# Attention and quantised FFN on one core: due times of a hand-planned instruction order, and two counters

## The chip, the cores and the metric

One NeuronCore of a Trainium2 chip runs the whole program in one launch. The metric is the device time of one execution in microseconds; lower is better. The time before is the median of three runs.

## The reference

`x` is 4 x 512 x 1024 (2048 tokens), a context of 64 more tokens goes with each of the 4 batches. With `LN` a layer norm without weights:

```python
n = LN(x);  hidden = concat([ctx, n], axis=1)              # 576 keys per batch
q = n @ Wq.T (16 heads of 96);  k, v = hidden @ Wk.T, hidden @ Wv.T (4 heads of 96, each for 4 q heads)
x = x + softmax(q k^T / sqrt(96)) v @ Wo.T
xq = fake_quant(LN(x), per row)
h = silu(xq @ fake_quant(w_gate).T) * (xq @ fake_quant(w_up).T)     # 2752 wide
x = x + fake_quant(h, per row) @ fake_quant(w_down).T
```

`fake_quant` scales each row by its largest magnitude over 127, rounds to whole numbers and scales back. Attention needs near-fp32 accuracy, so each fp32 operand is carried as two fp16 numbers (a high and a low part) and a product takes three matmuls.

## The kernel before

The program has two phases with a barrier of all engines between them. `attention_phase` (0 to 1248.6 us of the profile) does the attention of the four batches and, in its gaps, prepares the FFN weights; `ffn_phase` does the FFN on 16 tiles of 128 tokens.

**Attention.** A prologue is followed by four batches of 18 steps (`step_order`). Step j holds four score tiles `S` of head j (128 queries by 576 keys), five pieces `PV` of head j - 2, and side work `X`: projections V, Q, K and the output projection WO for this or the next batch. TensorE runs them in the order of `batch_order`. A score tile goes through a chain of engines: VectorE's row maximum (`max`, L1113), ScalarE's two exponentials (`exp`, L1006 and L1012; the second writes fp16 into `p_nat`, which has four slots, so it waits until the transposition of the same tile of the previous head has landed), GpSimd's low part (`low`, L791), and a DMA transposition `turn_p` (L686) into `pT`, which `PV` reads (L922). TensorE's next score tile but one waits for the exponentials. After the last tile of a head `invert` takes the reciprocals of the row sums, `inv_out` stores them to HBM (2 KB), `inv_in` (L697 is its wait) loads them back spread over 96 partitions, and `normalise` multiplies the head's output by them.

**Weights of the FFN.** 52 units (`("w", g)`), 4 during batch 0 and 16 during each of the others; every 13 units are 11 narrow ones (gate and up, 128 x 1024) and 2 wide ones (down, 128 x 2752, done in two halves). A unit is loaded into one of two buffers `w_in` (`stage`, L600); VectorE finds its row scale (`scale`, L1143 to L1154); ScalarE multiplies (`lift`, L976); VectorE takes the rounded numbers out into the one buffer `w_int` (`round`, L1161, which waits until the transposition of the piece before has read it, L1160); SP transposes (`turn`, L641) into `w_t` and stores (`keep`, L652, whose wait for the transposition is put down to that line). A wide piece takes all of `w_t`, so its `turn` also waits (L639) for the stores before it. In batch 0 the same two buffers also stage the fp32 query and output weights; `split` makes their high and low parts (ScalarE L962, VectorE L1066), and `cache` stores both for the later batches.

**The order.** Every engine runs one list in order, and a wait at its head holds all that is behind it. `pe_times` gives each TensorE operation a start and an end from fixed costs (`COST`, `S_COST`); `stage_events`, `token_events` and `engine_events` give every other step a due time as an offset from these; the steps of each engine are then sorted by due time. SP's list holds all DMAs of the attention phase. `weight_units` sets when units are due: unit i of batch b at `START[b] + (i + 0.4) * length / UNITS[b]`. Planned time is shorter than real time: batch 3 is planned from 786.7 to 1019.8, and its last output projection ends at 1232 us of the profile.

**Counters.** `w_up` (ScalarE) and `w_out` (VectorE) count both the lifts and rounds of units and the splits, so a wait on either is for a number in the joint order of `STAGE` (`ups`, `freed`).

**The end.** After its list SP waits for the last stores of `keep`. In `ffn_phase` TensorE spreads the scales (L1413) and ScalarE copies them (L1445); SP waits for the stores of `x2` (`store_x`, L722), loads the first token tile (L1307, `ln_tile`) and the quantised weights; VectorE normalises and quantises the tile (L1468 on), a transposition follows, and then the gate matmuls (L1391) start.

Of the kernel before, what the change touches and what calls it, by code (L numbers as in the profile page):

```python
# [1 line left out]

# [67 lines left out]
CUT = 11 * P  # L70
HALF = QC * D // 2
UNITS = (4, 16, 16, 16)

KEYS = [("K", c, h) for c in range(QC) for h in range(2)]
VALUES = [("V", ST - 1)] + [("V", s) for s in range(TT)]
# [112 lines left out]
def weight_units():  # L188

    g, units = 0, []  # L190
    for b in range(B):
        for i in range(UNITS[b]):
            units.append((START[b] + (i + 0.4) * (START[b + 1] - START[b]) / UNITS[b], ("w", g)))
            g += 1
    return units

# [20 lines left out]
    return halves_of(i[1] % NUNIT) if i[0] == "w" else 1  # L217


def ups(i, half=0):  # L220

    return sum(item_halves(k) for _, k in STAGE[:ITEM[i]]) + half + 1


def freed(n):
    return ups(STAGE[n][1], item_halves(STAGE[n][1]) - 1)


def smalls(g, k):
# [8 lines left out]
    return (k - parity + 1) // 2  # L238


def stage_events():

    act, dve, sp = [], [], []
    done = {}
    for n, (t, i) in enumerate(STAGE):
        if n < FIRST:
            done[n] = 0.0
            continue
        load = max(done[n - 2] + 1.0, t - 24.0)
        sp.append((load, "stage", n))  # L250
        t = max(t, load + 5.0)
        if i[0] == "w":
            g = i[1]
            if item_halves(i) == 1:
                dve += [(t, "scale", g, 0), (t + 6.0, "round", g, 0)]
                act.append((t + 3.0, "lift", g, 0))
                sp += [(t + 8.0, "turn", TURNS.index((g, 0))), (t + 12.0, "keep", TURNS.index((g, 0)))]
                done[n] = t + 6.5
            else:
                k = TURNS.index((g, 0))  # L260
                dve += [(t, "scale", g, 0), (t + 3.0, "scale", g, 1), (t + 9.0, "round", g, 0), (t + 15.0, "round", g, 1)]
                act += [(t + 6.0, "lift", g, 0), (t + 9.0, "lift", g, 1)]
                sp += [(t + 10.5, "turn", k), (t + 15.0, "keep", k), (t + 16.5, "turn", k + 1), (t + 21.0, "keep", k + 1)]
                done[n] = t + 15.5
        else:
            act.append((t, "split", n))
            dve.append((t + 2.5, "split", n))
            sp.append((t + 4.5, "cache", n))
            done[n] = t + 4.0
    return act, dve, sp  # L270


def token_events(b):

    q = filled_at(b, ("Q", KV - 1, QC - 1)) - 12.0
    act, dve, pool, sp = [], [], [], []
    for t in range(TT):
        s = q + 8.0 * t
        sp += [(s - 7.0, "tokens", b, t), (s + 11.0, "turn_tokens", b, t)]
        dve += [(s, "stats", b, t), (s + 4.0, "norm", b, t)]  # L280
        pool += [(s + 2.5, "power", b, t), (s + 8.0, "tokens_lo", b, t)]
        act.append((s + 5.5, "tokens_hi", b, t))
    sp.append((q + 25.0, "context", b))
    act.append((q + 31.0, "context_hi", b))
    pool.append((q + 32.5, "context_lo", b))
    return act, dve, pool, sp


def engine_events():

    act, dve, sp = stage_events()
    pool = []
    for b in range(B):
        for o in batch_order(b):
            t = END[b, o]
            if o[0] == "S":
                j, k = o[1:]
                dve.append((t + 0.1, "max", b, j, k))
                act.append((t + 1.0, "exp", b, j, k))
                pool.append((t + 3.0, "low", b, j, k))  # L300
                sp.append((t + 5.0, "turn_p", b, j, k))
                if k == TT - 1:
                    dve.append((t + 3.3, "invert", b, j))
                    sp += [(t + 3.8, "inv_out", b, j), (t + 6.5, "inv_in", b, j)]
            elif o[0] == "PV" and o[2] == TT:
                j = o[1]
                dve.append((t + 0.1, "normalise", b, j))
                act.append((t + 1.4, "out_hi", b, j))
                pool.append((t + 2.2, "out_lo", b, j))
                if HEADS[j % G] == G - 1:  # L310
                    sp.append((t + 4.0, "move_o", b, j // G))
            elif o[0] == "X" and o[2] == parts(o[1]) - 1:
                u = o[1]
                if u[0] == "WO":
                    dve.append((t + 0.1, "add", b, u))
                else:
                    act.append((t + 0.1, "evac", b, u))
                    dve.append((t + 1.6, "evac", b, u))
                if u[0] == "Q" and u[2] == QC - 1:
                    sp.append((t + 3.2, "move_q", b, u[1]))  # L320
                if u == ("WO", KV - 1, TT - 1, 0) or u == ("WO", KV - 1, TT - 1, 1):
# [12 lines left out]
    for n, (b, kv, h) in enumerate(OUT_USES):  # L334
        if b:
            sp.append((filled_at(*out_done(n - 2)) + 0.3, "out_w", n))
    return [sorted(e, key=lambda x: x[0]) for e in (act, dve, pool, sp)]


# [45 lines left out]
def attention_phase(nc, x, ctxT, wqT, wkT, wvT, woT, w_gu, w_dn, x2, inv_d, wq_c, wo_c, gu_q, dn_q, kept):  # L385
    with ExitStack() as ctx:
# [54 lines left out]
        e_in = [sem(f"e_in{i}") for i in range(2)]  # L441
        e_up = sem("e_up")
        e_out = sem("e_out")
        w_up = sem("w_up")
        w_out = sem("w_out")
        w_small = sem("w_small")
# [91 lines left out]
        def staged(eng, n):  # L538

            eng.wait_ge(w_in_s[n % 2], (n // 2 + 1) * EV)  # L540

        def split_to(n):

            kind, *a = STAGE[n][1]
            if kind == "wv":
                cols = slice(a[0] * HALF, (a[0] + 1) * HALF)
                return wv_hi[:, cols], wv_lo[:, cols]
            if kind == "q":
                slot = (a[0] * QC + a[1]) % 2
                return wq2[:, slot, 0, :], wq2[:, slot, 1, :]  # L550
            return wo2[:, a[1], 0, :], wo2[:, a[1], 1, :]
# [31 lines left out]
        def _(sp):  # L583
            def stage(n):

                if n >= 2:
                    sp.wait_ge(w_out, freed(n - 2))
                kind, *a = STAGE[n][1]
                if kind == "w":
                    q, u = divmod(a[0], NUNIT)  # L590
# [11 lines left out]
            def cache(n):  # L602

                kind, *a = STAGE[n][1]
                sp.wait_ge(w_out, freed(n))
                if kind == "q":
                    slot = (a[0] * QC + a[1]) % 2
                    sp.dma_start(wq_c[a[0], a[1]], wq2[:, slot, :, :]).then_inc(wq_kept[slot], EV)
                else:
                    sp.dma_start(wo_c[a[0], a[1]], wo2[:, a[1], :, :]).then_inc(wo_kept[a[1]], EV)  # L610
# [20 lines left out]
            def turn(k):  # L631

                g, h = TURNS[k]
                rows, _ = unit_part(g, h)
                sp.wait_ge(w_out, ups(("w", g), h))
                first, blocks = turn_blocks(k)
                sp.wait_ge(w_stored[k % 2], stores_before(k, k % 2) * EV)
                if blocks > KD or (k and turn_blocks(k - 1)[1] > KD):
# [170 lines left out]
        def _(pe):  # L809
# [31 lines left out]
            def v_proj(use, part, n):  # L841
                b, (_, s) = use
                if b is None:
                    if part == 0 and s < TT:
                        pe.wait_ge(xn_turned[s], EV)
                    elif s == ST - 1:
                        pe.wait_ge(ctx_lo, 1)
                        pe.wait_ge(w_out, freed(ITEM["wv", part]))
                if part == 0:
                    claim(use)  # L850
                rows = P if s < TT else C
# [6 lines left out]
            def q_proj(use, part, n):  # L858
                b, (_, kv, q) = use
                slot = (kv * QC + q) % 2  # L860
                if part == 0:
# [2 lines left out]
                    elif kv == 0 and q == 0:  # L864
                        pe.wait_ge(e_out, 1)
                    else:
                        pe.wait_ge(w_out, freed(ITEM["q", kv, q]))
                    if kv == 0 and q == 0:
                        for t in range(TT):
                            pe.wait_ge(xn_turned[t], EV if b is None else b * EV + 2 * EV)  # L870
# [6 lines left out]
            def out_proj(use, part, n):  # L877
# [4 lines left out]
                if t == 0:  # L882
                    if b:
                        pe.wait_ge(wo_in[h], ((b - 1) * KV + kv + 1) * EV)
                    else:
                        pe.wait_ge(w_out, freed(ITEM["o", kv, h]))
                claim(use)
                ts = slice(t * P, (t + 1) * P)
                ws = [slice(c * 512, (c + 1) * 512) for c in range(QC)]
# [57 lines left out]
        def _(act):  # L947
            DOWN = 1.0 / W_UP

            def w_split(n):  # L950
# [8 lines left out]
                elif kind == "o" and a[0]:  # L959
                    filled(act, out_done(a[0] * 2 + a[1] - 2))  # L960
                    act.wait_ge(wo_kept[a[1]], a[0] * EV)
                nc.scalar.activation(split_to(n)[0], split_from(n), ACT.Copy, scale=W_UP).then_inc(w_up, 1)  # L962

            def early_split(i):

# [94 lines left out]
        def _(dve):  # L1060
            DOWN = 1.0 / W_UP

            def w_split(n):
                hi, lo = split_to(n)
                dve.wait_ge(w_up, ups(STAGE[n][1]))
                nc.vector.scalar_tensor_tensor(lo, split_from(n), W_UP, hi, ALU.mult, ALU.subtract).then_inc(w_out, 1)  # L1066

            def early_split(i):
                dve.wait_ge(e_up, i + 1)
# [63 lines left out]
            def tile_scale(g, h):  # L1133
# [5 lines left out]
                if h == 0:  # L1139
                    staged(dve, n)  # L1140
                    if g:
                        dve.wait_ge(w_up, ups(("w", g - 1), halves_of((g - 1) % NUNIT) - 1))
                nc.vector.tensor_reduce(w_amax[0:rows, h:h + 1], w_in[0:rows, n % 2, cols], AX.X, ALU.max,  # L1143
                                        apply_absolute_value=True).then_inc(w_small, 1)
                if h < halves - 1:
# [10 lines left out]
            def round_off(g, h):  # L1156
                n, k = ITEM["w", g], TURNS.index((g, h))
                rows, cols = unit_part(g, h)
                dve.wait_ge(w_up, ups(("w", g), h))
                dve.wait_ge(w_turned, k * EV)  # L1160
                nc.vector.tensor_scalar(w_int[0:rows, 0:cols.stop - cols.start], w_in[0:rows, n % 2, cols], MAGIC, None,  # L1161
                                        ALU.subtract).then_inc(w_out, 1)
# [497 lines left out]
```

## Time and profile before

| | |
|---|---|
| median of three runs | 1757.22 us (1755.55 to 1758.23) |
| the profiled execution | 1757.65 us |
| its span, first to last instruction | 1755.9 us |
| TensorE matmul busy | 1567.4 us (89%) |
| VectorE, ScalarE, GpSimd busy | 1036.7, 655.3, 515.5 us |
| DMA moved | 323.6 MB, 77.2% of 16 engines' span |
| mean granted TensorE clock | 0.955 |

In the rows below, L12 is line 12 of the kernel. A timeline row gives start (us), busy time (us), engine, line, operation, what it writes and reads with its shape, and in brackets how long the engine sat idle before it and what ended that. For SP ("SPq") the second number is the time that the queue took to issue the DMA. A row of waits gives who waited for whom: us in total, times, longest. A row by stage gives the stretch, its length, busy us of TensorE's matmuls, its weight loads, VectorE, ScalarE and GpSimd (with counts), the mean granted TensorE clock, the mean busy share of the 16 DMA engines (over 1 where transfers overlap) and GB/s.

### The profile page before, as it was taken

The numbers are of one execution on the slowest core, as the hardware profiler recorded it, in microseconds if no ns is written. First come the engines' busy times: TensorE is split into PE (matmuls) and PEld (weight loads), VectorE is DVE, ScalarE is ACT, GpSimd is POOL, SyncE is SP. The second block draws the span as 40 slices with busy tenths as digits, with TensorE's granted clock in tenths as the row PEclk, the third lists the DMA queues.
The fourth block names the chain that finished last, engine by engine and source line by source line (L and its number), as shares of the span: only waits on it lengthen the run. The fifth ranks groups of instructions, "written<-read, shape, count | busy, mean of one in ns | idle before, by whom it ended". The sixth has DMA issues, their size and how long they took to land. (4 is left out here: it accounts for less than half of the span.)

```text
span 1755.9 us, 23588 instructions
## 1 busy us (share of the span) xinstructions
PE 1567.4 (89%) x8084; PEld 773.3 (44%) x8084; DVE 1036.7 (59%) x1760; ACT 655.3 (37%) x1180; POOL 515.5 (29%) x635
## 2 busy tenths in 40 slices
PE   6989989999877999888799788898579999999997
PEld 3544434654333465443346334443234444444443
DVE  5346554345555434555444445465379999898984
ACT  3456553256544225555422455452211111111110
POOL 3356653045445214445521244452000000000000
PEclk9999999999898999999999899999789999999998
DMA  7499999699999969999986999998863333324232
GB/s 233 116 249 237 240 231 233 185 212 228 226 227 230 200 173 222 239 209 230 222 200 187 263 218 205 207 202 199 263 227 85 91 89 86 95 80 105 70 93 64
DMA packets 546185, 323.62 MB, mean 184 GB/s; under 512 B 484144, under 2 KB 491056, under 8 KB 544944
## 3 DMA queue, kind: packets, MB, share of 16 engines
q1 hardware_dynamic: 546096, 322.49, 77.2%
q8 instruction: 50, 0.82, 0.2%
q14 instruction: 39, 0.32, 0.1%
HBM read 151.78 MB, written 46.79 MB: 113 GB/s over the span
## 5 line engine op out<-in xcount | busy, mean ns | idle before, releaser
L791 POOL TENSOR_TENSOR p_nat<-p_f,p_nat 128x512 f16<-128x512 f32 x256 | 300.6, 1174 | 478.9 <-ACT p_nat L1012 478.4
L1113 DVE TENSOR_REDUCE small<-ps_s 128x1 f32<-128x576 f32 x256 | 192.8, 754 | 257.2 <-PE ps_s L908 255.7
L907 PE MATMUL ps_s<-k,q 96*128 96x512 f16 x768 | 231.2, 393 | 95.4 <-ACT p_nat L1012 95.4
L1006 ACT ACTIVATE p_f<-ps_s,small 128x576 f32<-128x576 f32 x256 | 189.2, 739 | 267.5 <-DVE small L1113 265.5
L1012 ACT ACTIVATE p_nat<-ps_s,small 128x576 f16<-128x576 f32 x256 | 188.5, 736 | 133.3 <-DMA pT<-p_nat 132.7
L1391 PE MATMUL ps_gu<-w_gu_sb,xT 128*128 128x512 bf16 (+1 forms) x1152 | 230.8, 361 | 0.0
L1432 ACT ACTIVATE g_sb<-g_sb,sx 128x512 f32<-128x512 f32 (+1 forms) x128 | 74.5, 582 | 390.6 <-DVE g_sb L1503 331.5
L1404 PE MATMUL ps_d<-w_dn_sb,hT 128*128 128x512 bf16 x704 | 161.5, 383 | 5.4 <-DMA hT<-h_int 5.4
L907 PEld LDWEIGHTS ps_s<-k,q 96*128 96x128 f16 x768 | 76.2, 99 | 201.7 <-issue 82.1
L1391 PEld LDWEIGHTS ps_gu<-w_gu_sb,xT 128*128 128x128 bf16 x1152 | 112.8, 98 | 115.4
L922 PE MATMUL ps_o<-pT,v_lo 128*96 128x512 f16 x320 | 133.4, 417 | 33.0 <-DMA pT<-p_nat 32.9
L908 PE MATMUL ps_s<-k,q 96*128 96x64 f16 x768 | 150.1, 196 | 0.0
L818 PE MATMUL ps_g<-wo,o 128*128 128x512 f16 x384 | 148.9, 388 | 1.1 <-POOL o L797 1.1
L819 PE MATMUL ps_g<-wo,o 128*128 128x512 f16 x384 | 148.6, 387 | 0.0
L820 PE MATMUL ps_g<-wo,o 128*128 128x512 f16 x384 | 148.5, 387 | 0.0
L818 PE MATMUL ps_g<-xnT,wq 128*128 128x512 f16 x384 | 146.3, 381 | 1.4 <-DMA xnT<-xh 0.7
L820 PE MATMUL ps_g<-xnT,wq 128*128 128x512 f16 x384 | 146.2, 381 | 0.0
L819 PE MATMUL ps_g<-xnT,wq 128*128 128x512 f16 x384 | 146.1, 380 | 0.0
L1370 POOL TENSOR_TENSOR rstd<-var_eps,minus_half 128x1 f32<-128x1 f32 x16 | 8.8, 550 | 460.1 <-DVE var_eps L1473 460.1
L1174 DVE SCALAR_TENSOR_TENSOR x_acc<-ps_g,x_acc 128x512 f32<-128x512 f32 x128 | 88.1, 689 | 86.7 <-PE ps_g L820 86.5
L797 POOL TENSOR_TENSOR o<-o_tmp,o 96x512 f16<-96x512 f32 x64 | 75.6, 1182 | 194.8 <-ACT o L1021 194.8
L923 PE MATMUL ps_o<-pT,v_hi 128*96 128x512 f16 x320 | 130.1, 407 | 0.0
(113 smaller groups left out, 2403.6 us busy)
## 6 DMA issues: line engine op xcount, KB each, us to landing
w_in<-w_gu SPq DMA_DIRECT2D x40, 512.0 KB, 4.7
wq<-wq_c SPq DMA_DIRECT2D x36, 512.0 KB, 4.9
wo<-wo_c SPq DMA_DIRECT2D x24, 768.0 KB, 5.6
inv_sum<-inv_d SPq DMA_DIRECT2D x64, 192.0 KB, 3.4
gu_q<-w_t SPq DMA_DIRECT2D x44, 256.0 KB, 4.1
w_in<-w_dn SPq DMA_DIRECT2D x8, 1376.0 KB, 7.1
w_gu_sb<-gu_q SPq DMA_DIRECT2D x3, 2816.0 KB, 12.8
x_acc<-x SPq DMA_DIRECT2D x4, 2048.0 KB, 8.9
```

The costliest lines, as they stand in the source:

```text
L791: nc.gpsimd.tensor_tensor(n[:, S + C:2 * S], f[:, 0:T], n[:, 0:T], ALU.subtract)
L818: nc.tensor.matmul(o, l_hi, r_hi, start=(first and i == 0), stop=False)
L819: nc.tensor.matmul(o, l_hi, r_lo, start=False, stop=False)
L820: mm = nc.tensor.matmul(o, l_lo, r_hi, start=False, stop=(last and i == len(pairs) - 1))
L907: nc.tensor.matmul(o[:, 0:T], l, k2[0:HD, hl, kv, 0:T], start=(i == 0), stop=(i == 2))
L908: mm = nc.tensor.matmul(o[:, T:S], l, k2[0:HD, hl, kv, T:S], start=(i == 0), stop=(i == 2))
L922: nc.tensor.matmul(o, v_lo[:, t, kv, :], p[:, t, :], start=(t == 0), stop=False)
L1006: nc.scalar.activation(p_f[:, t % NF, :], scores(t), ACT.Exp, bias=bias, accum_out=sums[:, j % 2, t:t + 1])
L1012: nc.scalar.activation(p_nat[:, t % NN, 0:S], scores(t), ACT.Exp, bias=bias).then_inc(p_done, 1)
L1113: nc.vector.tensor_reduce(neg_max[:, j % 2, t:t + 1], scores(t), AX.X, ALU.max, negate=True).then_inc(mx_done, 1)
L1391: mm = nc.tensor.matmul(ps_gu[n % NR][:, 0:nu * P], xT[:, k, :], w[:, u0:u0 + nu, k, :], start=(k == 0), stop=(k == KD - 1))
L1404: mm = nc.tensor.matmul(ps_d[h][:], hT[0:rows, c, :], w_dn[0:rows, 4 * h:4 * h + 4, c, :], start=(c == 0), stop=(c == IC - 1))
```

## The change

Only due times and two counters change; every instruction of the computation stays.

- Splits count on new semaphores `h_up` and `h_out`; `w_up` and `w_out` count the units alone (`lifts`, `split_no`).
- A staged load is due `LAND` + 1 = 7 or more ahead of its first use (before 5); a split's `cache` comes 6 after it, 4.5 before.
- A `round` is due 6 or more after the `turn` before it; a `turn` 2.5 after its `round` and 6 after the stores it needs; a `keep` 6 after its `turn` (before: 4, or 4.5 for wide ones).
- `inv_in` is due 10 after the head's last score tile (before 6.5), 6.2 after `inv_out` (before 2.7).
- Token tiles of the next batch start 20 before the end of the query projections (before 12) in steps of 10 (before 8), with 8 between `stats` and `norm` (before 4).
- `out_w` 1.5 after the matmuls that free its buffer (before 0.3).
- In batch 3 the due times of the 16 units are drawn in to 0.85 of its length.

```diff
+WEIGHTS_FOR = (1.0, 1.0, 1.0, 0.85)
...
-            units.append((START[b] + (i + 0.4) * (START[b + 1] - START[b]) / UNITS[b], ("w", g)))
+            units.append((START[b] + (i + 0.4) * WEIGHTS_FOR[b] * (START[b + 1] - START[b]) / UNITS[b], ("w", g)))
...
-def ups(i, half=0):
-
-    return sum(item_halves(k) for _, k in STAGE[:ITEM[i]]) + half + 1
-
-
-def freed(n):
-    return ups(STAGE[n][1], item_halves(STAGE[n][1]) - 1)
+def lifts(g, half=0):
+
+    return sum(halves_of(i % NUNIT) for i in range(g)) + half + 1
+
+
+def split_no(n):
+
+    return sum(1 for _, i in STAGE[:n + 1] if i[0] != "w")
...
+LAND = 6.0
+TOKEN_LEAD, TOKEN_STEP = 20.0, 10.0
...
         load = max(done[n - 2] + 1.0, t - 24.0)
         sp.append((load, "stage", n))
-        t = max(t, load + 5.0)
-        if i[0] == "w":
-            g = i[1]
-            if item_halves(i) == 1:
-                dve += [(t, "scale", g, 0), (t + 6.0, "round", g, 0)]
-                act.append((t + 3.0, "lift", g, 0))
-                sp += [(t + 8.0, "turn", TURNS.index((g, 0))), (t + 12.0, "keep", TURNS.index((g, 0)))]
-                done[n] = t + 6.5
-            else:
-                k = TURNS.index((g, 0))
-                dve += [(t, "scale", g, 0), (t + 3.0, "scale", g, 1), (t + 9.0, "round", g, 0), (t + 15.0, "round", g, 1)]
-                act += [(t + 6.0, "lift", g, 0), (t + 9.0, "lift", g, 1)]
-                sp += [(t + 10.5, "turn", k), (t + 15.0, "keep", k), (t + 16.5, "turn", k + 1), (t + 21.0, "keep", k + 1)]
-                done[n] = t + 15.5
-        else:
+        t = max(t, load + LAND + 1.0)
+        if i[0] != "w":
+            t = split = max(t, split + 3.0)
             act.append((t, "split", n))
             dve.append((t + 2.5, "split", n))
-            sp.append((t + 4.5, "cache", n))
-            done[n] = t + 4.0
+            sp.append((t + 6.0, "cache", n))
+            done[n] = t + 5.0
+            continue
+        g, halves = i[1], item_halves(i)
+        t = max(t, lifted + 1.5)
+        for h in range(halves):
+            dve.append((t, "scale", g, h))
+            t += 3.0
+        for h in range(halves):
+            act.append((t, "lift", g, h))
+            t += 3.0
+        lifted = t
+        t -= 3.0 * (halves - 1)
+        for h in range(halves):
+            k = TURNS.index((g, h))
+            t = max(t, turned[-1] + LAND)
+            dve.append((t, "round", g, h))
+            wide = halves == 2 or (k and halves_of(TURNS[k - 1][0] % NUNIT) == 2)
+            t = max(t + 2.5, (kept[-1] if wide else kept[-2]) + LAND)
+            sp += [(t, "turn", k), (t + LAND, "keep", k)]
+            turned.append(t)
+            kept.append(t + LAND)
+        done[n] = t
...
-                    sp += [(t + 3.8, "inv_out", b, j), (t + 6.5, "inv_in", b, j)]
+                    sp += [(t + 3.8, "inv_out", b, j), (t + 10.0, "inv_in", b, j)]
...
-        s = q + 8.0 * t
-        sp += [(s - 7.0, "tokens", b, t), (s + 11.0, "turn_tokens", b, t)]
-        dve += [(s, "stats", b, t), (s + 4.0, "norm", b, t)]
-        pool += [(s + 2.5, "power", b, t), (s + 8.0, "tokens_lo", b, t)]
-        act.append((s + 5.5, "tokens_hi", b, t))
...
+        s = q + TOKEN_STEP * t
+        sp += [(s - 8.0, "tokens", b, t), (s + 16.0, "turn_tokens", b, t)]
+        dve += [(s, "stats", b, t), (s + 8.0, "norm", b, t)]
+        pool += [(s + 2.5, "power", b, t), (s + 12.0, "tokens_lo", b, t)]
+        act.append((s + 9.5, "tokens_hi", b, t))
...
-                    sp.wait_ge(w_out, freed(n - 2))
+                    freed(sp, n - 2)
...
-                nc.scalar.activation(split_to(n)[0], split_from(n), ACT.Copy, scale=W_UP).then_inc(w_up, 1)
+                nc.scalar.activation(split_to(n)[0], split_from(n), ACT.Copy, scale=W_UP).then_inc(h_up, 1)
```

## Rows read from the trace of the kernel before

**Rows 1.** Stages: us, PE PEld DVE ACT POOL busy, TensorE clock, DMA share, GB/s.
```profile
375.00:602.00 227.00, 192.84 (x972) 91.68 (x970) 115.96 (x184) 114.40 (x210) 109.95 (x136) 0.92 1.04 223
...
965.00:1200.00 235.00, 198.80 (x1032) 96.10 (x1030) 116.51 (x180) 120.56 (x225) 105.46 (x136) 0.93 1.01 219
1200.00:1249.00 49.00, 29.54 (x136) 13.49 (x135) 21.18 (x31) 6.74 (x7) 3.73 (x4) 0.89 0.67 190
```

**Rows 2.** Waits of the matmuls, whole span: total us, times, longest.
```profile
PE ps_s L907 <- ACT p_nat L1012: 95.4, 37, 7.2
PE ps_o L922 <- DMA pT<-p_nat: 32.9, 19, 4.4
```

**Rows 3.** Timeline of VectorE, end of attention and first FFN tile.
```profile
1232.81 0.69 DVE L1174 SCALAR_TENSOR_TENSOR x_acc<-ps_g,x_acc 128x512 f32<-128x512 f32 x1 [1.25 <-PE ps_g L820]
...
1240.07 0.86 DVE L1161 TENSOR_SCALAR w_int<-w_in 128x1344 bf16<-128x1344 f32 x1 [5.77 <-DMA w_t<-w_int]
...
1252.08 1.29 DVE L1468 BATCH_NORM_STATS2 stats<-x_ln 128x6 f32<-128x512 f32 x2 [3.30 <-DMA x_ln<-x]
```

**Rows 4.** Timeline of SP's queue over the same stretch: start, time to issue.
```profile
1233.53 0.38 SPq L722 DMA_DIRECT2D x<-x_acc  x1
...
1245.88 0.33 SPq L652 DMA_DIRECT2D dn_q<-w_t  x1
1248.79 0.33 SPq L1307 DMA_DIRECT2D x_ln<-x  x1
```

**Rows 5.** The chain of waits: first FFN matmuls.
```profile
1262.95 7.81 PE ps_gu L1391 x24
```

**Rows 6.** DMA issues: count, KB each, median us from issue to landing.
```profile
w_in<-w_dn SPq DMA_DIRECT2D x8, 1376.0 KB, 7.1
...
x<-x_acc SPq DMA_DIRECT2D x8, 1024.0 KB, 7.4
...
dn_q<-w_t SPq DMA_DIRECT2D x16, 352.0 KB, 3.5
...
w_t<-w_int SPq DMA_TRANSPOSE x60, 4.5
```

**Rows 7.** Waits of SP's queue, whole span.
```profile
SPq L697 <- DMA inv_d<-small: 40.9, 24, 4.9
...
SPq L652 <- DMA w_t<-w_int: 33.7, 18, 3.8
SPq L639 <- DMA dn_q<-w_t: 20.9, 10, 5.5
```

**Rows 8.** Waits of VectorE, whole span.
```profile
DVE w_int L1161 <- DMA w_t<-w_int: 49.6, 10, 11.0
```

**Rows 9.** VectorE's round of unit 37, batch 3; then the matmuls' waits, 985 to 1010 us.
```profile
999.71 0.86 DVE L1161 TENSOR_SCALAR w_int<-w_in 128x1344 bf16<-128x1344 f32 x1 [10.95 <-DMA w_t<-w_int]
...
PE ps_s L907 <- ACT p_nat L1012: 10.1, 2, 7.2
```

**Rows 10.** SP's queue just before it: start, time to issue.
```profile
986.84 0.55 SPq L679 DMA_DIRECT2D x_acc<-x  x1
987.48 6.79 SPq L686 DMA_TRANSPOSE pT<-p_nat  x1
```

**Rows 11.** ScalarE's split at 111 us; then the matmuls' waits, 100 to 116 us.
```profile
111.49 1.06 ACT L962 ACTIVATE wq<-w_in 128x1024 f16<-128x1024 f32 x1 [7.48 <-DMA w_in<-wqT]
...
PE ps_s L907 <- ACT p_nat L1012: 6.6, 2, 5.7
```

**Rows 12.** VectorE's round at 517 us; then the matmuls' waits, 505 to 535 us.
```profile
516.79 0.86 DVE L1161 TENSOR_SCALAR w_int<-w_in 128x1344 bf16<-128x1344 f32 x1 [5.75 <-DMA w_t<-w_int]
...
PE ps_s L907 <- ACT p_nat L1012: 7.3, 2, 4.6
```

**Rows 13.** VectorE's round at 764 us; then the matmuls' waits, 760 to 770 us.
```profile
763.77 0.86 DVE L1161 TENSOR_SCALAR w_int<-w_in 128x1344 bf16<-128x1344 f32 x1 [6.51 <-DMA w_t<-w_int]
...
PE ps_s L907 <- ACT p_nat L1012: 4.1, 1, 4.1
```

More of the change, by code:

```diff
@@ L238, in stores_before @@
     return (k - parity + 1) // 2
+LAND = 6.0
+TOKEN_LEAD, TOKEN_STEP = 20.0, 10.0
 def stage_events():
     act, dve, sp = [], [], []
-    done = {}
+    done, split, lifted, turned, kept = {0: 0.0, 1: 0.0, 2: 0.0, 3: 0.0}, 0.0, 0.0, [0.0], [0.0, 0.0]
     for n, (t, i) in enumerate(STAGE):
         if n < FIRST:
-            done[n] = 0.0
             continue
@@ L270, in stage_events @@
+        done[n] = t
     return act, dve, sp
 def token_events(b):
-    q = filled_at(b, ("Q", KV - 1, QC - 1)) - 12.0
+    q = filled_at(b, ("Q", KV - 1, QC - 1)) - TOKEN_LEAD
     act, dve, pool, sp = [], [], [], []
     for t in range(TT):
-        s = q + 8.0 * t
-        sp += [(s - 7.0, "tokens", b, t), (s + 11.0, "turn_tokens", b, t)]
-        dve += [(s, "stats", b, t), (s + 4.0, "norm", b, t)]
-        pool += [(s + 2.5, "power", b, t), (s + 8.0, "tokens_lo", b, t)]
-        act.append((s + 5.5, "tokens_hi", b, t))
@@ L283, in token_events @@
-    sp.append((q + 25.0, "context", b))
-    act.append((q + 31.0, "context_hi", b))
-    pool.append((q + 32.5, "context_lo", b))
+        s = q + TOKEN_STEP * t
[3 more added lines that the diff above has]
+        act.append((s + 9.5, "tokens_hi", b, t))
+    s = q + TOKEN_STEP * 2 + 16.0
+    sp.append((s, "context", b))
+    act.append((s + 8.0, "context_hi", b))
@@ L286, in token_events @@
+    pool.append((s + 9.5, "context_lo", b))
     return act, dve, pool, sp
@@ L335, in engine_events @@
         if b:
-            sp.append((filled_at(*out_done(n - 2)) + 0.3, "out_w", n))
+            sp.append((filled_at(*out_done(n - 2)) + 1.5, "out_w", n))
     return [sorted(e, key=lambda x: x[0]) for e in (act, dve, pool, sp)]
@@ L443, in attention_phase @@
         e_out = sem("e_out")
+        h_up = sem("h_up")
+        h_out = sem("h_out")
         w_up = sem("w_up")
@@ L540, in staged, with freed @@
             eng.wait_ge(w_in_s[n % 2], (n // 2 + 1) * EV)
+        def freed(eng, n):
+            kind, *a = STAGE[n][1]
+            if kind == "w":
+                eng.wait_ge(w_out, lifts(a[0], halves_of(a[0] % NUNIT) - 1))
+            else:
+                eng.wait_ge(h_out, split_no(n))
         def split_to(n):
@@ L604, in cache @@
                 kind, *a = STAGE[n][1]
-                sp.wait_ge(w_out, freed(n))
+                freed(sp, n)
                 if kind == "q":
@@ L634, in turn @@
                 rows, _ = unit_part(g, h)
-                sp.wait_ge(w_out, ups(("w", g), h))
+                sp.wait_ge(w_out, lifts(g, h))
                 first, blocks = turn_blocks(k)
@@ L847, in v_proj @@
                         pe.wait_ge(ctx_lo, 1)
-                        pe.wait_ge(w_out, freed(ITEM["wv", part]))
+                        freed(pe, ITEM["wv", part])
                 if part == 0:
@@ L866, in q_proj @@
                     else:
-                        pe.wait_ge(w_out, freed(ITEM["q", kv, q]))
+                        freed(pe, ITEM["q", kv, q])
                     if kv == 0 and q == 0:
@@ L885, in out_proj @@
                     else:
-                        pe.wait_ge(w_out, freed(ITEM["o", kv, h]))
+                        freed(pe, ITEM["o", kv, h])
                 claim(use)
@@ L1064, in w_split @@
                 hi, lo = split_to(n)
-                dve.wait_ge(w_up, ups(STAGE[n][1]))
-                nc.vector.scalar_tensor_tensor(lo, split_from(n), W_UP, hi, ALU.mult, ALU.subtract).then_inc(w_out, 1)
+                dve.wait_ge(h_up, split_no(n))
+                nc.vector.scalar_tensor_tensor(lo, split_from(n), W_UP, hi, ALU.mult, ALU.subtract).then_inc(h_out, 1)
             def early_split(i):
@@ L1141, in tile_scale @@
                     if g:
-                        dve.wait_ge(w_up, ups(("w", g - 1), halves_of((g - 1) % NUNIT) - 1))
+                        dve.wait_ge(w_up, lifts(g) - 1)
                 nc.vector.tensor_reduce(w_amax[0:rows, h:h + 1], w_in[0:rows, n % 2, cols], AX.X, ALU.max,
@@ L1158, in round_off @@
                 rows, cols = unit_part(g, h)
-                dve.wait_ge(w_up, ups(("w", g), h))
+                dve.wait_ge(w_up, lifts(g, h))
                 dve.wait_ge(w_turned, k * EV)
```

## The prediction

> **What bounds the kernel now.** I read the profile from its end. The chain of waits covers only the FFN: its first gate matmuls start at 1262.95 us [rows 5], and from there the chain is TensorE's own work, which the change does not touch. So two things can move: the time that attention takes, and the seam behind it.
>
> At the seam the reader is to see two ends. VectorE's last addition to `x_acc` starts at 1232.81 [rows 3] and SP stores the result at 1233.53 [rows 4]: attention proper is over. Yet the last half of the last weight unit is rounded only at 1240.07, after 5.77 us of waiting for the transposition of the half before [rows 3], its store is issued at 1245.88, and the FFN's first load follows at 1248.79 [rows 4]. The rounding of weights, and not attention, ends the first phase, about 12 us late.
>
> Inside attention the stages show TensorE with 192.8 busy us of 227 in the heads of batch 1 and 198.8 of 235 in those of batch 3, at a mean clock of 0.92 and 0.93 of full, while the 16 DMA engines stand at a share of 1.04 and 1.01; after 1200 us that falls to 0.67 [rows 1]. The matmuls wait 95.4 us for `p_nat`, written by ScalarE behind the transpositions, and 32.9 us for `pT` itself, 128.3 in all [rows 2]. Two causes stand behind these waits and the profile cannot part them by itself: full DMA engines, and lists in which something that nobody needs soon holds up something that TensorE needs. Of the second kind I see: SP waits 40.9 us for the reciprocals to land in HBM, 33.7 us for transposed weights and 20.9 us for stores of weights [rows 7], 95.5 together; VectorE waits 49.6 us in ten roundings of weights [rows 8].
>
> **The change, part by part.** It adds no instruction and no byte. Everything is a matter of place.
>
> *The seam.* Unit 15 of batch 3 was due at 786.7 + 15.4/16 x 233.1 = 1011.1 of the plan; with 0.85 it is 786.7 + 0.85 x 224.4 = 977.4, 34 earlier. The new spacing of wide pieces gives part back: a piece comes every 12 of the plan (6 from its turn to its keep, 6 from that to the next turn), and by the formula the last turn and keep come at 1012.5 and 1018.5 instead of 1027.6 and 1032.1. The plan ends at 1019.8, so the last keep now stands ahead of the last store of `x2`. What ends the phase is then the store at 1233.53. It is not enough that it is issued: the first load of the FFN waits for it to land. The median of its kind is 7.4 us, that of a 352 KB store of weights 3.5 [rows 6], so x2 is there between 1237 and 1241, and the load that was issued at 1248.79 [rows 4] goes out 8 to 12 us earlier; little else is under way there, which speaks for the longer end. Its data is awaited at once (3.30 us idle, VectorE starts at 1252.08 [rows 3]), and from it statistics, transposition and gates follow as before. I take **-10.5 us**. Bounds: -12.7, if the store's landing were hidden by the barrier (1248.79 to about 1236), and 0, if the heads stretch so far that they fill the room.
>
> *Roundings and splits.* Where a wait of this kind stops TensorE can be read at four places. A split waits 7.48 us for its load on ScalarE, and the matmuls near it lose 6.6 us [rows 11]. The second half of a wide unit waits 5.75 us and they lose 7.3 [rows 12]; 6.51 us and 4.1 [rows 13]; 10.95 us and 10.1 [rows 9]. Together 28.1 us. In the new order split 8 stands behind an exponential that it blocked (due 41.8 instead of 38.4, the exponential 39.1), and second halves are due 6 after the transposition they wait for, not 4.5. A weight transposition lands after 4.5 us in the median [rows 6], so 6 is enough for most and not for those that run beside a large load: at the worst place SP took 6.79 us merely to issue a transposition behind the 2 MB residual [rows 10], and only the order of the weight transposition (now 815.6, ahead of the residual's 816.7; before 817.6) is mended there, not the transfer. I take 12 of the 28.1: **-12 us**. Bounds 0 and -28; what is late next at these places is the score tile's own transposition.
>
> *SP's list.* `inv_in` moves 3.5 later; it stood 2.7 behind `inv_out` and now stands 6.2 behind, so most of the 40.9 us [rows 7] goes. `keep` goes from 4 to 6 behind its `turn`, and a wide `turn` from 1.5 behind the last keep to 6; most of 33.7 + 20.9 goes too. A good part of these waits lies in stretches where SP has nothing urgent behind it, and where DMA engines are full a DMA issued earlier mostly lands no earlier. No single place shows TensorE stopped by one of them, so I take little, 8 of the 95.5 us: **-8 us**, bounds 0 and, at half of TensorE's 128.3 us of waits [rows 2], -64. `inv_in` has cover: `normalise` needs it only two steps later, 16 after the last score tile against 10 plus a landing; if that cover goes, `ps_o` is freed late and the next PV waits.
>
> *Tokens, cache, out_w.* The loads of tokens come 1 earlier ahead of their statistics, `norm` 4 later behind them; The last is turned 9 of the plan before the query projections that read it (before 12), which is twice a transposition's 4.5 us [rows 6]: I count nothing, and up to 3 us a batch if that cover goes. The first `turn_tokens` now comes 4 ahead of the matmuls it waits for (before 1): SP then stands up to 4 us three times. Behind it is only the transposition of a score tile from the same time, so nothing is charged. The two counters cost nothing; they allow splits and units to pass each other in batch 0.
>
> *What it costs.* The heads of batch 3 now hold all 16 units. New there are the last 1376 KB load, three wide transpositions and about three stores. By time to landing that is 7.1 + 3 x 4.5 + 3 x 3.5 = 31 us [rows 6], but those overlap other transfers; by share they fall into DMA engines at 1.01 [rows 1], where each microsecond added may push the score transpositions back. Between 0 (all fill gaps) and 31 I take **+8 us**, nearer to the low end, since landing times are mostly latency.
>
> Sum: -10.5 - 12 - 8 + 8 = -22.5 us. Against the profiled execution, 1757.65, that is 1735.15; it stands 0.4 above the median of the runs, so I say **1735**.
>
> [...]
>
> **Rivals.**
> 1. *The DMA engines are the ceiling.* Waits leave SP and VectorE and come back as longer landings. For it: the share in all heads; against it: the places above where a single wait and TensorE's stop coincide. Then only the seam stays, less what the moved transfers cost: 1757.65 - 10.5 + 8 = 1755, within what can't be told from no change, or 1747 if they cost nothing.
> 2. *Slower: batch 3 is overfilled.* The two wide units of the end now fall among score transpositions. The nearest price is the one collision of a wide unit with a large load: the matmuls lost 10.1 us, and the clock fell with it [rows 9]. With each of the two units meeting such a stretch twice, and no relief elsewhere, 1757.65 - 10.5 + 4 x 10.1 = 1787; with one meeting each it is 1767. It is slower from the point where the heads of batch 3 stretch by more than 10.5 + 3.5 = 14 us.
> 3. *SP's list is the true limit.* Half of TensorE's waits go, 64 us instead of 20: 1757.65 - 10.5 - 64 + 8 = 1691. For it: SP takes 6.79 us for a single issue [rows 10], so its list can be full; against it: such an issue is itself a sign of full DMA engines.
> 4. *The order does not do it*: the last keep still ends the phase because wide units lag in real time. SP's relief alone, 1757.65 - 20 + 8 = 1746.
>
> **How the numbers follow.** My own case (1715 to 1749) gets 0.55, rival 1 0.16 (over half of it within 0.2%), rival 2 0.13, rival 3 0.07, rival 4 0.09. Rival 3's far end is left out below, the 1767 and 1787 above; the range is 1710 to 1758. A measurement of this kernel tells about 0.2% (3.5 us) from no change. Slower by more: 0.13; within: 0.10; faster by more: 0.77.
>
> **What would show it.** The last `keep` is issued before or within 3 us of the last store of `x2`, and the first gate matmuls start 10 us and more closer to the last addition (now 30.1 us). SP's wait for `inv_d` falls under 15 us, VectorE's for transposed weights under 25. TensorE's waits fall from 128 to about 105. If SP's waits go and TensorE's stay, rival 1 holds; if the stretch of batch 3's heads grows beyond 249 us, rival 2.

## The result, and the profile after

The changed kernel takes 1696.57 us (median of 4 runs, 1695.48 to 1700.98) against 1756.38 us of the kernel before measured with it: a ratio of 0.9664, 95% interval 0.9644 to 0.9684, or 59 us less by that ratio. Forecast were 1735 us and a range down to 1710; the direction held, the size did not. The profiled execution took 1700.98 us with a span of 1699.3.

First the seam. The timeline of VectorE in the changed kernel, from the last addition of the attention phase:

```profile
1187.91 0.69 DVE L1188 SCALAR_TENSOR_TENSOR x_acc<-ps_g,x_acc 128x512 f32<-128x512 f32 x1 [1.25 <-PE ps_g L834]
...
1196.20 1.29 DVE L1482 BATCH_NORM_STATS2 stats<-x_ln 128x6 f32<-128x512 f32 x2 [6.26 <-DMA x_ln<-x]
```

the timeline of SP's queue over the same stretch (start, time to issue):

```profile
1181.30 0.50 SPq L666 DMA_DIRECT2D dn_q<-w_t  x1
1188.63 0.39 SPq L736 DMA_DIRECT2D x<-x_acc  x1
1192.86 0.34 SPq L1321 DMA_DIRECT2D x_ln<-x  x1
```

and from the chain of waits, the first gate matmuls:

```profile
1206.82 7.37 PE ps_gu L1405 x24
```

The last addition came at 1232.81 [rows 3] and comes at 1187.91: attention is 44.9 us shorter. From it to the gates it was 30.1 us [rows 3, 5] and is 18.9: the seam is 11.2 us shorter. The last keep (1181.30) is now ahead of the last store (1188.63), as the plan said, and the FFN's first load follows 4.2 us behind that store. 44.9 + 11.2 = 56.1, and the profiled executions differ by 56.7. So all of it lies in these two places, and four fifths of the gain lie in attention, where I had expected half.

Attention itself, from the start to the last addition, in rows by stage (columns as in rows 1), before and after:

```profile
0.00:1232.81 1232.81, 1087.54 (x5792) 548.57 (x5792) 611.92 (x941) 571.59 (x1032) 506.66 (x619) 0.95 0.94 215
```

```profile
0.00:1187.91 1187.91, 1076.57 (x5792) 546.59 (x5792) 617.66 (x942) 569.60 (x1032) 511.01 (x619) 0.96 0.96 225
```

The same 5792 matmuls were busy 11.0 us less, at a granted clock of 0.96 instead of 0.95; TensorE's idle time fell by the other 33.9 us. A quarter of what attention gained is thus clock, for which the forecast had no term.

The waits of the matmuls, whole span (total us, times, longest):

```profile
PE ps_s L921 <- ACT p_nat L1026: 68.1, 25, 7.1
PE ps_o L936 <- DMA pT<-p_nat: 20.2, 16, 5.7
```

128.3 us [rows 2] have become 88.3. By stage, the heads of batches 1 and 3 (columns as in rows 1):

```profile
370.00:580.00 210.00, 189.01 (x971) 91.06 (x970) 118.28 (x185) 115.11 (x213) 113.58 (x138) 0.95 1.09 242
925.00:1150.00 225.00, 201.04 (x1057) 98.31 (x1055) 126.01 (x194) 124.55 (x231) 106.34 (x136) 0.93 1.08 247
```

Batch 1's heads run as many matmuls (971 for 972) in 210 us instead of 227 [rows 1], at a clock of 0.95 instead of 0.92, and the DMA share has risen from 1.04 to 1.09 and the rate from 223 to 242 GB/s; in batch 3 the rate went from 219 to 247, there with more of the weight units in the stretch. A share of 1.04 had not meant that the engines could do no more. The score transpositions land a little later than before (median 4.8 us for 4.4), and still TensorE waits less.

The waits of SP's queue, then of VectorE:

```profile
SPq L666 <- DMA w_t<-w_int: 12.0, 7, 3.5
...
SPq L653 <- DMA dn_q<-w_t: 6.0, 2, 4.0
...
SPq L711 <- DMA inv_d<-small: 0.4, 1, 0.4
```

```profile
DVE w_int L1175 <- DMA w_t<-w_int: 52.4, 17, 7.1
...
DVE o_tmp L1145 <- DMA inv_sum<-inv_d: 33.9, 12, 7.4
```

SP's three waits were 40.9 + 33.7 + 20.9 us [rows 7] and are 0.4 + 12.0 + 6.0. VectorE's roundings wait as long as before, 52.4 us against 49.6 [rows 8], though they wait 17 times and at most 7.1 us, not 10 times and up to 11.0. That already contradicts the part of the forecast that was built on them.

One more of SP's waits changed, which neither the rows ahead of the forecast nor the forecast looked at: the wait of `out_w` for the matmuls that free its buffer, before and after.

```profile
SPq L629 <- PE ps_g L820: 43.4, 11, 7.4
```

```profile
SPq L643 <- PE ps_g L834: 15.8, 5, 7.4
```

Before, it was SP's largest wait of the attention phase in total, larger than that for the reciprocals.

### The profile page after: what moved, and what is told of

The parts are those of the page before. It is cut to its first block and busy times, and to the rows that moved or that the text cites. A ratio compares the mean times of both kernels' runs of the same rounds, so it can differ in the third digit from the quotient of the medians.

```text
span 1699.3 us, 23588 instructions
## 1 busy us (share of the span) xinstructions
PE 1554.6 (91%) x8084; PEld 770.8 (45%) x8084; DVE 1040.9 (61%) x1760; ACT 653.1 (38%) x1180; POOL 519.8 (31%) x635
## 5 line engine op out<-in xcount | busy, mean ns | idle before, releaser
L921 PE MATMUL ps_s<-k,q 96*128 96x512 f16 x768 | 227.1, 387 | 68.3 <-ACT p_nat L1026 68.1
L1446 ACT ACTIVATE g_sb<-g_sb,sx 128x512 f32<-128x512 f32 (+1 forms) x128 | 74.6, 583 | 393.1 <-DVE g_sb L1517 335.1
L1026 ACT ACTIVATE p_nat<-ps_s,small 128x576 f16<-128x576 f32 x256 | 188.3, 736 | 37.9 <-DMA pT<-p_nat 37.7
L936 PE MATMUL ps_o<-pT,v_lo 128*96 128x512 f16 x320 | 132.0, 413 | 20.3 <-DMA pT<-p_nat 20.2
```

Of the source, the lines that this page charges most:

```text
L921: nc.tensor.matmul(o[:, 0:T], l, k2[0:HD, hl, kv, 0:T], start=(i == 0), stop=(i == 2))
L936: nc.tensor.matmul(o, v_lo[:, t, kv, :], p[:, t, :], start=(t == 0), stop=False)
L1026: nc.scalar.activation(p_nat[:, t % NN, 0:S], scores(t), ACT.Exp, bias=bias).then_inc(p_done, 1)
```

## The experiments

Three theories. **L**: SP's list was the limit; what holds it holds the score transpositions behind it. Its strong form says that SP has no time to spare at all. **W**: the gain is the new distances of the weight units. **M**: moved transfers meet by luck; parts have no price of their own. Percentages are of the kernel before measured on the same chip, and 1% is 17.6 us.

**The reciprocals alone (e1_inv_only), and all but them (e2_no_inv).**

```diff
-                    sp += [(t + 3.8, "inv_out", b, j), (t + 6.5, "inv_in", b, j)]
+                    sp += [(t + 3.8, "inv_out", b, j), (t + 10.0, "inv_in", b, j)]
```

That is the first, in the kernel before; the second takes the same line back in the changed one.

> The kernel before (1757 us) with inv_in alone due 10 instead of 6.5 after the head's last score tile. Theory L (SP's list was the limit, and its longest hold was the wait for the reciprocals, 40.9 us): 20 us or more of the change's 60, so 1737 us or less, with SP's wait for inv_d near 0 and ScalarE's wait for pT well under the 132.7 us of before. Theory W (the gain comes from the new distances of the weight units): within 5 us of 1757. Theory M (moved DMAs meet by chance in a better way, no part has a price of its own): anything between, and not in proportion to the wait removed.

> The changed kernel (1697 us) with inv_in alone put back to 6.5. L: 1717 us or more, SP's wait for inv_d back near 40 us. W: within 5 us of 1697, though the wait is back.

Alone: 1742.0 us, ratio 0.9896 (0.9857 to 0.9936), 18.3 us less. Taken back: 1719.7 us, 0.9767 (0.9732 to 0.9803), 18.1 us more than the change. W falls as the whole of the cause, and M has its first evidence against it: the part has a price clear of noise in both surroundings. Each price carries some 6 us of doubt, so that they agree to 0.2 us is luck. L's own 20 us were just missed. The waits of ScalarE's second exponential for the transpositions, in the kernel before

```profile
ACT p_nat L1012 <- DMA pT<-p_nat: 132.7, 67, 8.1
```

and in e1:

```profile
ACT p_nat L1012 <- DMA pT<-p_nat: 58.8, 32, 5.0
```

SP's wait for the reciprocals, 40.9 us [rows 7], became

```profile
SPq L697 <- DMA inv_d<-small: 2.5, 5, 1.5
```

38.4 us of SP's waiting went with 73.9 us of ScalarE's and 18.3 us of time. TensorE itself waited only 11.8 us less; the table below takes that up.

**The wait without the move (e8_hold_only).**

```diff
+                    sp += [..., (t + 6.5, "hold", b, j), (t + 10.0, "inv_in", b, j)]
...
+            def hold(b, j):
+                sp.wait_ge(inv_out_s, (head(b, j) + 1) * EV)
```

> The changed kernel, inv_in still issued at 10, but at 6.5 SP also waits, without a DMA, until the reciprocals have landed in HBM. Theory L: the wait itself is the cost, so this is as slow as putting inv_in back (1720 us, 0.9767 of before), with ScalarE's wait for pT near 83 us. If instead the place of the 192 KB load among the transpositions is what cost, this stays within 5 us of 1697.

1712.7 us, 0.9746 (0.9715 to 0.9777): 14.4 us slower than the change, of the 18.1 that the full move is worth. No transfer is added, taken away or reordered against the changed kernel, so most of the price is the wait itself. SP's waits for `inv_d` are 41.4 us in all, put down to what stands behind the hold, most of it to score transpositions:

```profile
SPq L699 <- DMA inv_d<-small: 27.1, 18, 4.1
```

ScalarE's wait for the transpositions, which I expected near 83 us, was only

```profile
ACT p_nat L1030 <- DMA pT<-p_nat: 42.8, 32, 4.3
```

so the path from the held list to TensorE is not the one I had named, or not it alone. What reaches TensorE is in the table below; by which engine it comes stays open.

**How late is too late (e12_inv_late, e14_inv_8).** The changed kernel with `inv_in` due 13 and 8.5.

> The changed kernel with inv_in due 13 after the last score tile. SP's wait is gone already (0.4 us), so L sees no further gain; VectorE's normalise already waits 33.9 us for inv_sum and would wait more: 1700 to 1712 us. If it is faster, the place of the load among the transpositions has a price of its own.

> The changed kernel with inv_in due 8.5. Between the two prices now known (SP waits 39.6 us for the reciprocals at 6.5 and the kernel is 18 us slower; VectorE waits 101.2 us for inv_sum at 13 and it is 26 us slower) there is a best place. SP's wait should come back in part (5 to 12 us, 2 to 6 us of time) and VectorE's fall from 33.9 to about 20: 1692 to 1702 us. If the two are one cost seen twice, the sum is flat: within 3 us of 1697.

13 gave 1725.3 us, 0.9810 (0.9782 to 0.9838), 25.6 us slower than 10, more than expected; the wait of `normalise` in VectorE's list, 33.9 us at 10, became

```profile
DVE o_tmp L1145 <- DMA inv_sum<-inv_d: 101.2, 27, 10.0
```

67 us more of it, while SP waits no less. 8.5 gave 1699.2 us, 0.9671 (0.9645 to 0.9696), no different from 10: SP waits 4.0 us for the reciprocals, VectorE 15.5 for `inv_sum`. The place has a flat floor between 8.5 and 10 and steep sides at 6.5 and 13.

**The weight units (e5_stage_only, e9_wide_close, e6_keep_early, e13_loads_late).** First the due times of loads, splits, rounds, turns and keeps alone, with the two counters:

> Of the change only the due times of loads, splits, rounds, turns and keeps and the two counters; inv_in at 6.5, units spread over batch 3, tokens and out_w as before. If the parts add up, what is left after the reciprocals (18 to 22 us of 60) and the drawn-in units (14) is 25 us, less what tokens and out_w do: 1757 - 20 to - 28, so 1729 to 1737 us. Theory L: SP's waits for w_t and dn_q fall from 54.6 to about 20 us, ScalarE's wait for pT from 132.7 to about 95. Theory M: under 1747 is not reached, the parts only work together.

1741.6 us, 0.9904 (0.9870 to 0.9939): 16.9 us less, 5 us above the range that adding up gave. Then one distance at a time taken out of the changed kernel:

```diff
e9_wide_close
-            t = max(t + 2.5, (kept[-1] if wide else kept[-2]) + LAND)
+            t = t + 2.5
e6_keep_early
-            sp += [(t, "turn", k), (t + LAND, "keep", k)]
+            sp += [(t, "turn", k), (t + 4.0, "keep", k)]
e13_loads_late
-        t = max(t, load + LAND + 1.0)
+        t = max(t, load + 5.0)
```

> The changed kernel, but a turn is due 2.5 after its round whatever stores it waits for, so that the pieces of wide units are 8.5 apart instead of 12. Theory L: SP waits for dn_q (6.0 us) again for 15 to 20 us and the kernel loses 4 to 8 us: 1701 to 1705. If the gain of the due times of the stage (17 us alone) is chiefly this distance, 1708 or more; if it has no price, within 3 us of 1697.

> The changed kernel with each keep due 4 instead of 6 after its turn, all else in place. L: SP waits for w_t again (12.0 goes back to 25 or more) and the kernel loses in the proportion that the reciprocals showed (about 22 us for 40 us of waiting): 5 to 10 us, so 1702 to 1707. M: no price, within 3 us of 1697.

> The changed kernel with a staged load due only 5 ahead of its use, as before, not 7. In batch 0 the splits wait for loads on ScalarE and VectorE again, in front of exponentials and maxima: if that is the price, 3 to 8 us, so 1700 to 1705, all of it in batch 0 and at the wide units. If loads have room anyway, within 3 us of 1697.

e9: 1713.6 us, 0.9759 (0.9733 to 0.9784), 16.7 us slower, nearly all that the weight units are worth. Its SP waits for the stores, 6.0 us in the changed kernel, are

```profile
SPq L653 <- DMA dn_q<-w_t: 25.9, 11, 4.4
```

e6: 1695.5 us, 0.9646 (0.9613 to 0.9679): no price; 6.9 us more of SP's waiting for `w_t` came with 4.3 us less for `dn_q`. e13: 1704.2 us, 0.9696 (0.9671 to 0.9722): 5.6 us, about the width of its interval. L had expected 1702 to 1707 for e6, but SP's waits for landings there came to 20.6 us against 19.6, so that it hardly tests L. Of the three distances tried, one counted, the one in front of a wide `turn`. Taking it out does more than bring the wait back: by the kernel's own due times it also puts 25 of the 60 weight transpositions 1.3 to 14 earlier, closer together. No run parts the wait from the crowding, as e8 did for the reciprocals. The distance of a `round` behind the `turn` before it was not tried alone.

**Batch 3's units spread out again (e3_units_spread).** `WEIGHTS_FOR` all 1.0.

> The changed kernel with batch 3's units spread over its whole length again (1.0 for 0.85). The seam from the last output projection to the first gate matmuls grows from 19.3 us to 30 or more, since the last keep is then about 12 later than before in the plan; attention up to the last output projection gets shorter by up to 8 us if filling batch 3 cost anything. All theories: 1697 + 11 - 8 to + 22, so 1700 to 1719 us.

1713.1 us, 0.9742 (0.9714 to 0.9770), 13.7 us slower. SP's queue at the end:

```profile
1184.94 0.39 SPq L736 DMA_DIRECT2D x<-x_acc  x1
...
1199.69 0.33 SPq L666 DMA_DIRECT2D dn_q<-w_t  x1
1202.55 0.34 SPq L1321 DMA_DIRECT2D x_ln<-x  x1
```

Without the drawing-in, the last store is issued 3.7 us earlier (1184.94 for 1188.63): that is what filling batch 3 costs in these two profiles. The last keep is issued at 1199.69 and the FFN's first load 9.7 us later than in the changed kernel. From the last addition (1184.22) to the gates (1216.55) it is 32.3 us, 13.4 more than there. That is nearly the whole difference of the medians, 13.7, so by these runs filling batch 3 costs from about nothing to some 4 us. The 0.85 alone in the old distances (e4_units_drawn_only) has no time: with those due times the engines' lists wait for one another in a circle.

**The tokens (e7_old_tokens, e15_norm_close).** All due times of the tokens as before; then only those inside a tile (`norm` 4, `tokens_hi` 5.5, `tokens_lo` 8, `turn_tokens` 12 after `stats`), with the new lead and step.

> The changed kernel with the tokens' due times of before. My prediction charged nothing: within 3 us of 1697. If the norm that waits for GpSimd holds VectorE's maxima, 1700 to 1705.

> The changed kernel with the tokens' lead and step kept (20 and 10) but the distances inside a tile as before (norm 4, tokens_hi 5.5, tokens_lo 8, turn_tokens 12 after stats). Old tokens cost 9 us. If the wait of norm for GpSimd (VectorE's list held) was the price, this costs most of it: 1702 to 1707. If it was lead and step (a tile's steps each get more room), within 3 us of 1697.

e7: 1708.2 us, 0.9717 (0.9685 to 0.9749), 9.3 us slower, where I had charged nothing. e15: 1717.6 us, 0.9771 (0.9746 to 0.9795), 18.8 us slower, worse than the old times. `norm` hardly waits for GpSimd in it (5.8 us in all, 4.7 in the changed kernel); what grew, from 29.1 us in the changed kernel, is the wait for the next tile's load in front of `stats`:

```profile
DVE stats L1092 <- DMA xc<-x: 49.5, 7, 10.0
```

`turn_tokens` of tile t is then due at the same time as the load of tile t + 2. That this is why the load comes late is argued, not shown. A second hold is new in e15, SP's in front of the first `turn_tokens` of a batch, which waits for the last query projections: 19.7 us, three times, up to 7.4. It is due 8 ahead of the end of these matmuls, where the changed kernel has 4 and the old times 1, and neither the changed kernel nor e7 shows such a wait. So e15 has a cost that is its own, and it does not tell which of the old times costs the 9 us of e7. There `stats` waited only 16.5 us; `norm` waited for GpSimd 8.0 us more than in the changed kernel, which is a candidate and not shown.

**The strong form of L (e11_out_on_act).** The 64 stores of the reciprocals go out from ScalarE's queue.

```diff
-            def inv_out(b, j):
-                sp.wait_ge(inv_done, head(b, j) + 1)
-                sp.dma_start(inv_d[j], inv_col[:, j % 2, :]).then_inc(inv_out_s, EV)
+            def inv_out(b, j):
+                act.wait_ge(inv_done, head(b, j) + 1)
+                act.dma_start(inv_d[j], inv_col[:, j % 2, :]).then_inc(inv_out_s[j % 2], EV)
```

> The changed kernel with the 64 stores of the reciprocals issued by ScalarE instead of SP. Nothing else moves and the bytes are the same. Theory L in its strong form (SP's list has no time to spare, so its issues count like its waits): 64 issues of about 0.4 us and 10.2 us of waiting for invert leave SP, and 64 issues enter a ScalarE that is busy for 38%: 8 to 15 us faster, 1682 to 1689. Theory D (the DMA engines are full, and only waits with an empty queue behind them cost): within 4 us of 1697, or slower if ScalarE's own list is now held by the reciprocal.

1696.3 us, 0.9660 (0.9636 to 0.9684), against the changed kernel's 0.9664. 64 issues fewer in SP's list, and 10.2 us fewer of waiting for `invert`, bring nothing that shows; its runs spread from 1687.5 to 1700.7. ScalarE's list is now held in their place, 28.6 us in front of exponentials, while its wait for the row maxima fell from 320.0 to 290.1 us, so a small gain may hide behind that hold. What SP does with its time says more: before a score transposition it waits for tiles that GpSimd has not finished, 35.6 us in the kernel before (18 times), 48.1 in the changed one (31 times) and 63.0 in e11 (44 times). At those times SP is ahead of the tiles and not behind them: it is not out of time. The Trainium skill (DMA: Bandwidth & Descriptors, "Issuing engines are not separate DMA queues") says that issuing from another engine saves only the issuer's time; this run agrees, with a difference of 0.04%, within an interval of 0.24% to either side.

**Together (e16_combo).** e11 with `inv_in` at 9 and `keep` at 4.

> The changed kernel with the reciprocals stored by ScalarE, inv_in at 9 and keep 4 after its turn. From the runs: 0 for the first, 0 to -3 for the second, -3 for the third: 1688 to 1697 us.

1690.0 us, 0.9631 (0.9604 to 0.9657): 6 us under the changed kernel by the ratios, and the two intervals overlap, so it is no slower and perhaps a little faster.

**Where the waiting arrives.** One profiled execution each, in us; ScalarE's column is the second exponential's wait for transpositions, the next three are TensorE's.

| run | ScalarE waits | waits for `p_nat` | waits for `pT` | busy (8084 matmuls) | execution |
|---|---|---|---|---|---|
| before | 132.7 | 95.4 | 32.9 | 1567.4 | 1757.65 |
| e1_inv_only | 58.8 | 89.5 | 27.0 | 1561.1 | 1742.10 |
| e12_inv_late | 19.5 | 86.0 | 19.1 | 1566.8 | 1728.94 |
| e2_no_inv | 83.2 | 74.8 | 24.9 | 1564.7 | 1722.68 |
| e8_hold_only | 42.8 | 74.6 | 23.6 | 1562.0 | 1718.58 |
| e9_wide_close | 59.8 | 67.9 | 33.3 | 1553.6 | 1711.85 |
| changed | 37.7 | 68.1 | 20.2 | 1554.6 | 1700.98 |

Between e2, e8, e9 or e12 and the changed kernel, the differences of TensorE's three columns add up to that of the execution within 1 us; between e1 and the kernel before they give 18.1 for 15.6. So these three are the account. ScalarE's wait does not follow the time: e12 has the least of it and is slower than four of the others. And the busy time is no constant, though the matmuls are the same. In the kernel before, TensorE was busy without a gap from 960 to 985 us at a granted clock of 1.00, and busy for 15.0 us of the next 25, at 0.78. (The forecast told that the clock fell there and named rows 9, which do not show it; these numbers are from the same trace.) Of the differences in execution that e1, e2, e8 and e12 show, 40 to 47% are matmuls that took longer. In e9 none is.

## Why the prediction was wrong

*The seam* was priced at -10.5 and measured -11.2 us: right, by the mechanism given. *Filling batch 3* was priced at +8 and cost 3.7 in two profiles, and not more by e3's medians. Together -2.5 was forecast where the profiles show -7.5. In e3, where the keeps have the new spacing and the units are spread, the seam is 32.3 us long; so the drawing-in is worth 13.4 at the seam, and the new spacing of wide pieces alone lengthened it by 2.2. By e3's medians the 0.85 is worth 13.7 net (its profiled execution is 10.0 above that of the changed kernel, which was the slowest of four).

*The two counters and `out_w`* were priced at nothing and were not tried alone. For `out_w` that is a gap: SP's wait for it fell by 27.6 us, more than any but the reciprocals'. The other parts add up without it (below), which speaks for a small price, but a price of 10 us would be lost in their intervals.

*Roundings and splits*, -12 us, is the first step that failed. I read the four places where VectorE waited for a weight transposition, or ScalarE for a load, while TensorE stood still, and took the one for the cause of the other. VectorE's wait for `w_t` did not fall (49.6 to 52.4 us) while TensorE's fell by 40; in e5 it even rose to 67.2 us in a kernel that is 16.9 us faster. The long SP issue of 6.79 us [rows 10] stood beside one of them, and I take it that both were late together, which no run shows. Nor was that issue a matter of the 2 MB residual alone: the transposition just ahead of the residual, at 979.62 us, took 7.13 us to issue, behind a load of 2816 KB.

*SP's list*, -8 us, is the term that was mis-sized, by a factor of four. "No single place shows TensorE stopped by one of them" was true of the rows I read and wrong as a reason: 52 holds of 1.8 us on average and up to 5.5 [rows 7] shift the score transpositions behind them, and reach TensorE spread out, as waits and as a lower granted clock, not at one place. The other reason, that where DMA engines are full a DMA issued earlier mostly lands no earlier, did not hold either: in batch 1's heads the same bytes moved at 242 GB/s for 223. The runs give 18 us for the reciprocals (38 to 39 us of SP's wait) and 17 for the distance before a wide turn (20 us of it): 0.5 and 0.8 us of time for each microsecond of waiting, the second with the crowding in it. The forecast had 8 for 95.5, or 0.08.

*The clock* had no term. 11.0 of the 44.9 us of attention are the same matmuls run faster, as told above; they are part of the prices of the runs and do not come on top.

*Tokens*, priced at nothing, gave 9.3 us. Taken out one by one the parts give 18.1 (reciprocals) + 16.7 (wide turns) + 5.6 (loads) + 13.7 (drawn-in units) + 9.3 (tokens) - 3.2 (keeps) = 60.2 us, for 59 measured. Each of the six carries some 6 us, so a sum that comes out to 1 us is luck; that it comes out within 10 or so speaks against M a second time. Put together from the runs on both sides (e5's 16.9, the reciprocals, the drawn-in units and the tokens) it is 58.0.

*Of the rivals*, the DMA ceiling fell: the heads got 17 us shorter at a higher share. Batch 3 was not overfilled. Rival 3 named the right resource and nearly the right time (1691), but its reason, that SP's list is full, has e11 and SP's waits for score tiles against it: what it stands still for counted, and not how much it does. That its time came close is partly luck, for it had TensorE's waits fall by 64 us, where they fell by 40 and the clock gave 11. I gave it 0.07 and left it out of the range because "full DMA engines" explained the same rows. A row of the kernel before would have told the two apart: SP's 35.6 us in front of score tiles that were not ready.

Of the signs I had named, the last keep's place, the seam and SP's wait for `inv_d` came true; VectorE's wait for transposed weights did not fall under 25 us, and TensorE's waits fell to 88 and not to about 105.

## What to carry to other kernels

In a list that one engine issues in order, price each hold by what stands behind it, not by whether the bottleneck is seen to stop at it: here a microsecond of SP's waiting for reciprocals was worth 0.5 us of the kernel, and one of waiting in front of a wide transposition up to 0.8. That is no fixed rate: the 10.2 us that e11 took out of SP's list brought nothing that shows, and the wait for `out_w` was never priced. List every wait of such an engine, those for other engines too and not only those for DMAs. A due time that allows for the landing it waits for takes the wait away; for the reciprocals it left 25.7 us more of VectorE's waiting for `inv_sum` (8.2 to 33.9) and the kernel was still 18 us faster. Moving a step later has a far side too, where its reader's list is held: find both sides (6.5 and 13 here) and stand between. A DMA share of 1 is not proof of full engines; the new order raised it from 1.04 to 1.09 and the rate from 223 to 242 GB/s. And count TensorE's busy time with its waits: here 33.9 us less idle time came with 11.0 us less busy time, at a higher granted clock.

## What was not expected of the hardware

The share and rate of the DMA engines rose with the same transfers and the same sizes (1.04 to 1.09, 223 to 242 GB/s in batch 1's heads). A store of 2 KB whose landing SP waits for held its list for up to 4.9 us [rows 7].
